# A graph layer on one core: the slot one-hots computed on VectorE instead of ScalarE, and a third batch in the ring of cross one-hots

## The chip, the cores and the metric

The kernel runs on one core of one Trainium2 chip. The metric is the device time of one launch in microseconds (us). The kernel before took 1250.79 us, the median of three runs (1250.07 to 1251.7).

## What is computed

One layer of a graph network with 3125 nodes of 256 features and 53,125 edges (`src`, `dst`, `edge_weight`). In the reference, cut to what matters:

```python
xn = _layernorm(x)
x = x + gnn(xn, src, dst, edge_weight, W, b) + linear_attention_block(xn, ...)
x = x + top2_of_16_experts(_layernorm(x), ...)
# gnn: msgs = edge_weight[:, None] * xn[dst]; agg = segment_sum(msgs, src, 3125); agg @ W.T + b
# attention block: q, k, v; elu + 1; message; norm; 512-wide relu MLP; norm
```

The change lies in the graph part: the sum of the edges' messages over their nodes, and the sorting of edges that comes before it.

## The kernel before, in words

All five engines run their own instruction streams and meet at semaphores. TensorE is called PE, VectorE DVE, ScalarE ACT, GpSimd POOL and SyncE SP in the profile.

There are three stages. In the **first** (to about 118 us), x is normalised, y = xn W is stored to DRAM, and `keys` makes the attention's keys tile by tile: PE multiplies (`project_k`, line 784), ACT makes the exponential in two operations (`exp_keys`, L468 and L470), DVE adds the positive part (L1249) and sums (L1242), PE accumulates (`sum_xk`, L802). There are 25 such tiles. The **middle stage** (about 118 to 785 us) has 13 groups, g = 0 to 12, and each covers 32 edge columns and two tiles of 128 nodes of the dense attention block. The **last stage** is the experts.

A group of the middle stage has 56 steps. In steps 0 to 31 PE multiplies a one-hot matrix (`hot`) by 128 gathered rows of y (L964), and DVE adds the result from PSUM to the node sums in SBUF (`evict_row`, L1319). Steps 32 to 55 are 24 "cross" steps for bins that a tile of edges shares with the next: PE multiplies `cross_hots` by the same rows (L973), and DVE adds two results at a time (`evict_pair`, L1325, at odd steps from 33). DVE makes `hot` eight at a time (L1312), six steps ahead. PE may be four PSUM banks, that is eight row steps, ahead of DVE's evictions. POOL gathers the rows with indirect DMAs (L702), and ACT scales them by the edge weights (`scale_rows`, L530).

Beside these steps each engine has other work, placed at fixed step numbers in a function `beside` of PE and one of DVE, and in a list written out by hand on ACT:

- The dense block of the group: PE's L852 (query), L865 (attend), L876 (turn), L885 (merge), L895 (hidden, at steps 19 to 29) and L904 (`down`, at steps 34 and 35); ACT's `hidden_relu` (L523), of which the second half must be there before PE's step 34; DVE's statistics, centring (L1393) and adding (L1400).
- The sorting of the edges of group g + 2 (`sorts`, so in groups 0 to 10; groups 0 and 1 are sorted in the first stage between the keys). DVE finds each edge's place (L1122 to L1154), splits it into a tile number and a slot number, marks the tile (`mark_tiles`, `in_tile`, L1169, at steps 21, 27, 31, 37) and multiplies the mark by the edge's fields (`make_record`, L1179, at steps 24, 30, 36, 43), eight columns at a time. ACT makes the slot one-hots of the same eight columns (`slot_hot`, L413 and L415): eight operations Abs(iota - slot), one for each column, and one Relu(1 - that). PE multiplies the two (`reorder`, L758, at steps 33, 40, 46, 54). A batch is called k = 0 to 3.
- The cross one-hots (`cross_hot`, L427 and L429) are made by ACT in the same manner, in three batches of eight for each group, into a ring of two batches. So batch 2 of a group can only be written once PE has used batch 0 of the same group (step 39).

On ACT the order in a group, around the change, is: `cross_hot(g, 0)`, scaling, `cross_hot(g, 1)`, `hidden_relu(g, 0)`, scaling twice, `slot_hot(g+2, 0)`, `hidden_relu(g, 1)`, the query's exponential with two table loads, `slot_hot(g+2, 1)`, `slot_hot(g+2, 2)`, `std(1, g)`, `cross_hot(g, 2)`, `slot_hot(g+2, 3)`, scaling three times, `message_turned(g+1)`.

Of the kernel before, what the change touches and what calls it, by code (L numbers as in the profile page):

```python
# [16 lines left out]
P = 128  # L17
# [6 lines left out]
def gps_layer(nc, x, src, dst, edge_weight, gnn_W, gnn_b, Wq, Wk, Wv, Wm, W1, W2, g1, b1, g2, b2,  # L24
# [47 lines left out]
    with ExitStack() as ctx:  # L72
# [3 lines left out]
        def sem(name):  # L76
            return ctx.enter_context(nc.semaphore(name))
# [45 lines left out]

        first_use = sb("first_use", [P, 5 * COLS])
        assert 2 * BATCH * P <= 5 * COLS
# [3 lines left out]
        cross_hots = first_use[:, 0:2 * BATCH * P].rearrange("p (b c) -> p b c", c=P)  # L129
        pieces = sb("pieces", [P, COLS // 2, FIELDS, 2], BF16)  # L130
# [20 lines left out]
        record = [sb(f"record{k}", [P, CH // 2, FIELDS, GT, 2], BF16) for k in range(2)]  # L151
        in_slot = [sb(f"in_slot{k}", [P, CH, P], BF16) for k in range(2)]
        place_b = sb("place_b", [P, GE], BF16)
        place_i = sb("place_i", [P, 3, GE], I32)
        place_f = sb("place_f", [P, GE])
        ends = sb("ends", [BINS, 1])
# [96 lines left out]
        gathered = [[sem(f"gathered{h}_{q}") for q in range(GT // GC)] for h in range(2)]  # L253
        places_ready, slot_hot_ready = sem("places_ready"), sem("slot_hot_ready")
        d_q, d_exp, d_elu, d_att, d_msg = sem("d_q"), sem("d_exp"), sem("d_elu"), sem("d_att"), sem("d_msg")
# [142 lines left out]
        def _(act):  # L398
# [8 lines left out]

            def slot_hot(g, k):
                act.wait_ge(places_ready, g + 1)
                if g * CHUNKS + k >= 2:  # L410
                    act.wait_ge(reordered, g * CHUNKS + k - 1)
                for c in range(CH):
                    act.activation(in_slot[k % 2][:, c, :], iota[:, :], ACT.Abs, bias=place_f[:, k * CH + c:k * CH + c + 1])  # L413
                act.drain()  # L414
                act.activation(in_slot[k % 2][:, :, :], in_slot[k % 2][:, :, :], ACT.Relu, scale=-1.0, bias=1.0).then_inc(slot_hot_ready, 1)  # L415


            def cross_hot(g, b):
                k = g * (CROSS // BATCH) + b
                act.wait_ge(picks_kept, g + 1)  # L420
                if b == 2:
                    act.wait_ge(met, g * STEPS + GT + BATCH)
                elif g >= 1:
                    act.wait_ge(met, (g - 1) * STEPS + GT + (b + 2) * BATCH)
                its = slice(k % 2 * BATCH, (k % 2 + 1) * BATCH)
                for j in range(BATCH):
                    act.activation(cross_hots[:, k % 2 * BATCH + j, :], iota[:, :], ACT.Abs, bias=picked[g % 2][:, b * BATCH + j:b * BATCH + j + 1])  # L427
                act.drain()
                act.activation(cross_hots[:, its, :], cross_hots[:, its, :], ACT.Relu, scale=-1.0, bias=1.0).then_inc(cross_hot_ready, 1)  # L429
# [56 lines left out]
            for t in range(NT):  # L486
                exp_keys(t)
                if t in (1, 3, 5, 7):
# [51 lines left out]
            for g in range(NG):  # L540
                sorts = g + 2 < NG
                more = g + 1 < NG
                if g == 0:
                    scale_rows(0, 2)
                    keep_list(1)
                    scale_rows(0, 3)
                    message_turned(0)
                    scale_rows(0, 4)
                    std(0, 0)
                    first_scaled(0)  # L550
                    scale_rows(0, 5)
                    n1_turned(0)
                    scale_rows(0, 6)
                    scale_rows(0, 7)
                if g >= 1:
                    scale_rows(g, 6)
                    scale_rows(g, 7)
                    std(0, g)
                if g >= 1 and more:
                    keep_list(g + 1)  # L560
                if g >= 1:
                    first_scaled(g)
                    n1_turned(g)
                cross_hot(g, 0)
                if more:
                    scale_rows(g + 1, 0)
                cross_hot(g, 1)
                hidden_relu(g, 0)
                if more:
                    scale_rows(g + 1, 1)  # L570
                    scale_rows(g + 1, 2)
                if sorts:
                    slot_hot(g + 2, 0)
                hidden_relu(g, 1)
                if more:
                    act.preload_act_table(ACT.Exp)
                    query_exp(g + 1)
                    act.preload_act_table(ACT.Sqrt)
                if sorts:
                    slot_hot(g + 2, 1)  # L580
                    slot_hot(g + 2, 2)
                std(1, g)
                cross_hot(g, 2)
                if sorts:
                    slot_hot(g + 2, 3)
                if more:
                    scale_rows(g + 1, 3)
                    scale_rows(g + 1, 4)
                    scale_rows(g + 1, 5)
                    message_turned(g + 1)  # L590
# [48 lines left out]
        def _(pool):  # L639
# [28 lines left out]
            pool.iota(bin_no[:, :, :], [[1, BINS], [0, GE]], base=0, channel_multiplier=0, allow_small_or_imprecise_dtypes=True)  # L668
            pool.iota(tile_of[:, :, :], [[1, GT], [0, 2]], base=0, channel_multiplier=0, allow_small_or_imprecise_dtypes=True)
            pool.iota(tile_start[:, :], [[P, GT]], base=0, channel_multiplier=0, allow_small_or_imprecise_dtypes=True)  # L670
            pool.drain().then_inc(consts_ready, 1)
# [61 lines left out]
        def _(pe):  # L733
# [18 lines left out]
            def reorder(g, k):  # L752
                pe.wait_ge(record_ready, g * CHUNKS + k + 1)
                pe.wait_ge(slot_hot_ready, g * CHUNKS + k + 1)
                if k == 0:
                    pe.matmul(bins_of_tiles, ones[0:BINS, :], meets[:, :], start=True, stop=True)
                for c in range(CH):
                    last = pe.matmul(in_order, in_slot[k % 2][:, c, :], record[k % 2][:, c // 2, :, :, c % 2].rearrange("p f t -> p (f t)"),  # L758
                                     start=(k == 0 and c == 0), stop=(k == CHUNKS - 1 and c == CH - 1))
                last.then_inc(reordered, 1)  # L760
# [189 lines left out]
            def add_up(g):  # L950
# [16 lines left out]
                for b in range(CROSS):  # L967
# [3 lines left out]
                    if b % 2 == 0:  # L971
                        pe.wait_ge(evicted, evictions_before(g, unit))
                    pe.matmul(bank_of(g, unit)[:, (b % 2) * C:(b % 2 + 1) * C], cross_hots[:, (g * CROSS + b) % (2 * BATCH), :],  # L973
                              rows[h][:, bass.ds(row_of[b], 1), :].rearrange("p t c -> p (t c)"),
# [115 lines left out]
        def _(dve):  # L1090
# [57 lines left out]
            def split_places(g):  # L1148
# [15 lines left out]
            def mark_tiles(g, k):  # L1164
                own = slice(k * CH, (k + 1) * CH)
                dve.drain()
                whole = [P, CH // 2, GT, 2]
                two = place_b[:, own].rearrange("p (a b) -> p a b", b=2)
                dve.tensor_tensor(in_tile[:, :, :, :], two.unsqueeze(2).to_broadcast(whole), tile_of[:, :, :].unsqueeze(1).to_broadcast(whole),  # L1169
                                  ALU.is_equal)  # L1170

            def make_record(g, k):
                dve.drain()
                if g * CHUNKS + k >= 2:
# [228 lines left out]
            def beside(g, step):  # L1403
# [327 lines left out]
```

## Time and profile before

| | |
|---|---|
| median of three runs | 1250.79 us (1250.07 to 1251.7) |
| profiled execution, first to last instruction | 1249.4 us |
| PE, DVE, ACT, POOL busy | 1089.0, 800.6, 675.8, 610.4 us |
| mean granted TensorE clock | 0.946 |
| a window of the middle stage, 190 to 707 us: PE, DVE, ACT, POOL busy | 478.71, 441.56, 446.89, 337.56 of 517 us |

For the profiled execution the span is the time on record; no launch time of its own is given with it. It is 1.39 us below the median of the runs. A busy share says how long an engine executed, not whether something else waited for it. An engine can also be unable to go faster with idle time in its row, where its own instructions wait for each other.

### The profile page before, as it was taken

To read this page: it belongs to the slowest core of one execution; us is meant where nothing else is said; L and a number is where in the kernel's file an instruction comes from. 1 tells how busy PE (TensorE), PEld (TensorE's weight loads), DVE (VectorE), ACT (ScalarE), POOL (GpSimd) and SP (SyncE) were. 2 spreads that over 40 slices of the span, in tenths; PEclk is the share of its full clock that TensorE was granted. 3 is DMA by queue.
4 is the path that set the end of the run, shared out by engine and by line. 5 is a ranking of instruction groups with operands and counts; after the bars stand their busy time and mean duration, and the time that the engine had idled before them with its cause. 6 is when DMAs were issued, how large, how long until landed. Compare 5 with 4: busy or idle time off the path is not lost.

```text
span 1249.4 us, 21035 instructions
## 1 busy us (share of the span) xinstructions
PE 1089.0 (87%) x6272; PEld 933.1 (75%) x6272; DVE 800.6 (64%) x1896; ACT 675.8 (54%) x1630; POOL 610.4 (49%) x625
## 2 busy tenths in 40 slices
PE   6797789999999999989999998716999999999990
PEld 5675677777777777767777787306999999999980
DVE  7875678888888888888888877673222222222226
ACT  4568697898978979789797874311011011011000
POOL 5937556575675766757557570002333333333320
PEclk9898899999999999999999999767999999999995
DMA  7214222232222322223223230325999999999958
GB/s 221 87 35 123 68 72 81 72 93 77 85 85 72 93 74 84 89 71 92 76 81 89 75 102 7 103 95 176 335 325 334 331 335 330 330 334 333 335 170 307
DMA packets 113487, 196.08 MB, mean 157 GB/s; under 512 B 13506, under 2 KB 61440, under 8 KB 113408
## 3 DMA queue, kind: packets, MB, share of 16 engines
q1 hardware_dynamic: 84073, 120.62, 28.8%
q0 software_dynamic: 26112, 71.34, 18.2%
q10 hardware_dynamic: 3222, 3.20, 0.7%
q8 instruction: 33, 0.54, 0.2%
q14 instruction: 47, 0.38, 0.1%
HBM read 177.12 MB, written 17.99 MB: 156 GB/s over the span
## 4 chain that ended last, share of the span: by engine, by line
PE 48%; DVE 14%; ACT 14%; issue 6%; DVEq 6%; POOL 6%; DMA 3%; ACTq 3%; SPq 0%; POOLq 0%
PE psum L1058 19%; PE psum L1068 9%; PE psum L964 7%; ACT in_slot L413 6%; POOL arena L702 5%; PE psum L973 3%; DVE agg L1319 2%; ACT first_use L427 2%; PE psum L895 2%; DMA arena<-y_rows,gather_i 2%; DVE agg L1325 2%; PE psum L885 2%; DVE agg L1700 1%; ACTq L414 1%; ACT arena L530 1%
## 5 line engine op out<-in xcount | busy, mean ns | idle before, releaser
L702 POOL DMA_INDIRECT arena<-y_rows,gather_i x416 | 437.5, 1052 | 250.9 <-PE psum L964 78.2
L964 PE MATMUL psum<-arena,hot 128*128 128x256 f32 x832 | 218.3, 393 | 14.9 <-issue 6.5
L635 ACT ACTIVATE arena<-psum 128x512 f32<-128x512 f32 x64 | 38.2, 597 | 327.6 <-PE psum L1058 327.6
L1319 DVE TENSOR_TENSOR agg<-psum,agg 128x256 f32 x416 | 174.6, 420 | 55.1 <-DVE agg L1319 31.0
L964 PEld LDWEIGHTS psum<-arena,hot 128*128 128x128 f32 x832 | 151.3, 192 | 49.7 <-issue 26.8
L1058 PEld LDWEIGHTS psum<-arena 128*128 128x128 f32 x1536 | 181.2, 194 | 4.9 <-issue 2.5
L530 ACT ACTIVATE arena<-arena,listed 128x256 f32<-128x256 f32 x416 | 172.6, 495 | 21.7 <-DMA arena<-y_rows,gather_i 21.7
L1058 PE MATMUL psum<-arena 128*128 128x128 f32 x1536 | 181.7, 277 | 2.0 <-DVE arena L1657 2.0
L973 PE MATMUL psum<-arena,first_use 128*128 x624 | 161.0, 394 | 25.2 <-ACT first_use L429 24.8
L1664 DVE TENSOR_TENSOR arena<-psum,arena 128x512 f32<-128x512 f32 x64 | 44.2, 691 | 204.8 <-PE psum L1058 204.8
L718 POOL DMA_INDIRECT chosen_rows<-arena,back_at x64 | 63.3, 988 | 219.7 <-DVE arena L1671 215.0
L973 PEld LDWEIGHTS psum<-arena,first_use 128*128 128x128 f32 x624 | 115.4, 196 | 48.8 <-issue 35.1
L413 ACT ACTIVATE in_slot<-iota,place_f 128x128 bf16<-128x128 f32 x416 | 126.6, 387 | 4.4 <-DVE place_f L1154 4.2
L713 POOL DMA_INDIRECT xnT<-n_rows,count x64 | 62.1, 970 | 121.8 <-DVEq L1651 101.6
L1325 DVE TENSOR_TENSOR agg<-psum,agg 128x512 f32<-128x512 f32 x156 | 105.8, 678 | 23.4 <-issue 13.4
L427 ACT ACTIVATE first_use<-iota,picked 128x128 f32<-128x128 f32 x312 | 94.9, 389 | 0.0
L1068 PE MATMUL psum<-arena 128*128 128x256 f32 x384 | 90.8, 379 | 0.0
L1068 PEld LDWEIGHTS psum<-arena 128*128 128x128 f32 x384 | 69.2, 190 | 7.4
L1671 DVE COPY arena<-psum 128x256 f32<-128x256 f32 x64 | 27.2, 424 | 60.7 <-PE psum L1068 60.7
L1312 DVE TENSOR_TENSOR hot<-iota,node_in_bin 128x1024 f32<-128x1024 f32 x52 | 63.0, 1212 | 2.5 <-issue 2.5
L1058 PEld LDWEIGHTS psum<-arena,xnT 128*128 128x128 f32 x512 | 59.7, 192 | 0.8
L1179 DVE TENSOR_TENSOR record<-in_tile,pieces 128x1792 bf16<-128x1792 bf16 x52 | 57.3, 1102 | 4.7
(227 smaller groups left out, 1634.7 us busy)
## 6 DMA issues: line engine op xcount, KB each, us to landing
arena<-in_L_ffn_w_dram SPq DMA_DIRECT2D x144, 512.0 KB, 5.8
xnT<-in_L_ffn_w_dram SPq DMA_DIRECT2D x48, 512.0 KB
arena<-y_rows,gather_i POOLq DMA_INDIRECT x416, 2.8
arena<-chosen_rows SPq DMA_DIRECT2D x4, 1280.0 KB, 9.9
y_rows<-w ACTq DMA_DIRECT2D x6, 512.0 KB, 2.9
agg<-in_x_dram SPq DMA_DIRECT2D x4, 640.0 KB, 6.6
n_rows<-arena SPq DMA_DIRECT2D x4, 640.0 KB
out_dram<-agg SPq DMA_DIRECT2D x4, 640.0 KB
```

The source lines that it names most:

```text
L413: act.activation(in_slot[k % 2][:, c, :], iota[:, :], ACT.Abs, bias=place_f[:, k * CH + c:k * CH + c + 1])
L427: act.activation(cross_hots[:, k % 2 * BATCH + j, :], iota[:, :], ACT.Abs, bias=picked[g % 2][:, b * BATCH + j:b * BATCH + j + 1])
L530: last = act.activation(rows[h][:, t, :], rows[h][:, t, :], ACT.Copy, scale=weight[h][:, t:t + 1])
L702: pool.indirect_dma_start(rows[h][:, t, :], None, y_rows, bass.IndirectOffsetOnAxis(ap=gather_i[h][:, t:t + 1], axis=0)).then_inc(gathered ...
L718: pool.indirect_dma_start(chosen_rows, bass.IndirectOffsetOnAxis(ap=back_at[:, n:n + 1], axis=0), e_y[:, n % WS, :], None)\
L964: pe.matmul(bank_of(g, t // 2)[:, (t % 2) * C:(t % 2 + 1) * C], hot[:, (g * GT + t) % HOTS, :], rows[h][:, t, :], start=True, stop=True).t ...
L973: pe.matmul(bank_of(g, unit)[:, (b % 2) * C:(b % 2 + 1) * C], cross_hots[:, (g * CROSS + b) % (2 * BATCH), :], rows[h][:, bass.ds(row_of[b ...
L1058: last = pe.matmul(bank[b][:, m * P:(m + 1) * P], w[s][:, k * EH + m * P:k * EH + (m + 1) * P], e_xT[:, h, k * P:(k + 1) * P], start=(k == ...
L1068: last = pe.matmul(bank[6 + h][:, 0:C], e_hid[:, h, k * P:(k + 1) * P], e_w3[s][:, k * C:(k + 1) * C], start=(k == 0), stop=(k == EHC - 1))
L1312: dve.tensor_tensor(hot[:, first:first + BATCH, :], iota[:, :].unsqueeze(1).to_broadcast([P, BATCH, P]), node_in_bin[g % 2][:, t:t + BATCH ...
L1319: dve.tensor_tensor(own, bank_of(g, t // 2)[:, (t % 2) * C:(t % 2 + 1) * C], own, ALU.add).then_inc(evicted, 1)
L1325: dve.tensor_tensor(own, bank_of(g, GT // 2 + a), own, ALU.add).then_inc(evicted, 1)
```

## The change

1. The slot one-hots move from ACT to DVE. `slot_hot` with its nine ACT operations for eight columns goes. `mark_slots` does the same eight columns in one DVE comparison of 16-bit values, laid out in pairs of columns as `in_tile` already is. Its constant operand `slot_no` is made once by POOL. In groups 0 to 10 it stands at DVE's steps 26, 29, 38 and 44. In the first stage it stands between `mark_tiles` and `make_record` of each batch.
2. The negated float copy of the slot numbers (`place_f`, L1154) goes; `place_b` now holds tile and slot numbers, and one cast writes both.
3. The ring of `cross_hots` holds three batches, so a whole group; a batch waits only for the same batch of the group before. `cross_hot(g, 2)` moves on ACT from behind `std(1, g)` to before `hidden_relu(g, 1)`, into the place of `slot_hot(g+2, 0)`.

```diff
-        first_use = sb("first_use", [P, 5 * COLS])
+        first_use = sb("first_use", [P, CROSS * P])
...
-        in_slot = [sb(f"in_slot{k}", [P, CH, P], BF16) for k in range(2)]
-        place_b = sb("place_b", [P, GE], BF16)
+        in_slot = [sb(f"in_slot{k}", [P, CH // 2, P, 2], BF16) for k in range(2)]
+        slot_no = sb("slot_no", [P, P, 2], BF16)
+        place_b = sb("place_b", [P, 2, GE], BF16)
...
             def cross_hot(g, b):
-                if b == 2:
-                    act.wait_ge(met, g * STEPS + GT + BATCH)
-                elif g >= 1:
-                    act.wait_ge(met, (g - 1) * STEPS + GT + (b + 2) * BATCH)
+                if g >= 1:
+                    act.wait_ge(met, (g - 1) * STEPS + GT + (b + 1) * BATCH)
...
                 if t in (1, 3, 5, 7):
-                    slot_hot(0, t // 2)
...
-                if t in (19, 20, 22, 24):
-                    slot_hot(1, (19, 20, 22, 24).index(t))
...
-                if sorts:
-                    slot_hot(g + 2, 0)
+                cross_hot(g, 2)
                 hidden_relu(g, 1)
...
-                if sorts:
-                    slot_hot(g + 2, 1)
-                    slot_hot(g + 2, 2)
                 std(1, g)
-                cross_hot(g, 2)
-                if sorts:
-                    slot_hot(g + 2, 3)
...
-                dve.tensor_copy(place_b[:, :], place_i[:, 1, :])
-                dve.tensor_scalar(place_f[:, :], place_i[:, 2, :], -1.0, None, ALU.mult).then_inc(places_ready, 1)
+                dve.tensor_copy(place_b[:, :, :], place_i[:, 1:3, :])
...
+            def mark_slots(g, k):
+                if g * CHUNKS + k >= 2:
+                    dve.wait_ge(reordered, g * CHUNKS + k - 1)
+                whole = [P, CH // 2, P, 2]
+                two = place_b[:, 1, k * CH:(k + 1) * CH].rearrange("p (a b) -> p a b", b=2)
+                dve.tensor_tensor(in_slot[k % 2][:, :, :, :], two.unsqueeze(2).to_broadcast(whole), slot_no[:, :, :].unsqueeze(1).to_broadcast(whole),
+                                  ALU.is_equal).then_inc(slot_hot_ready, 1)
...
             def make_records(g, k):
                 mark_tiles(g, k)
+                mark_slots(g, k)
                 make_record(g, k)
...
+                if step == 26 and sorts:
+                    mark_slots(g + 2, 0)
+                if step == 29 and sorts:
+                    mark_slots(g + 2, 1)
+                if step == 38 and sorts:
+                    mark_slots(g + 2, 2)
+                if step == 44 and sorts:
+                    mark_slots(g + 2, 3)
```

## Rows read from the trace of the kernel before

**Rows 1.** The page: each engine's busy time, share and instructions.

```profile
PE 1089.0 (87%) x6272; PEld 933.1 (75%) x6272; DVE 800.6 (64%) x1896; ACT 675.8 (54%) x1630; POOL 610.4 (49%) x625
```

**Rows 2.** Busy by stretch: PE, PEld, DVE, ACT, POOL, clock, DMA share, GB/s.

```profile
190.00:707.00 517.00, 478.71 (x2367) 390.70 (x2366) 441.56 (x1050) 446.89 (x1090) 337.56 (x320) 0.98 0.28 82
346.68:398.30 51.62, 48.45 (x238) 39.80 (x237) 44.13 (x106) 44.77 (x109) 33.40 (x33) 0.97 0.28 82
709.04:750.84 41.80, 40.06 (x189) 33.25 (x188) 30.70 (x71) 29.19 (x69) 31.64 (x32) 1.00 0.34 99
```

**Rows 3.** PE's waits, 190 to 707 us: total, times, longest.

```profile
PE psum L973 <- ACT first_use L429: 21.1, 10, 2.2
PE psum L964 <- issue: 5.8, 10, 0.6
```

**Rows 4.** DVE's waits, 190 to 707 us: total, times, longest.

```profile
DVE agg L1319 <- DVE agg L1319: 22.0, 99, 0.6
DVE agg L1325 <- issue: 13.4, 10, 1.5
DVE agg L1319 <- PE psum L964: 9.7, 39, 0.7
```

**Rows 5.** Timeline of DVE: start, duration, instruction, and idle time before it.

```profile
350.13 0.42 DVE L1319 TENSOR_TENSOR agg<-psum,agg 128x256 f32 x1 [0.21 <-PE psum L964]
350.47 1.22 DVE L1312 TENSOR_TENSOR hot<-iota,node_in_bin 128x1024 f32<-128x1024 f32 x1
351.61 0.42 DVE L1319 TENSOR_TENSOR agg<-psum,agg 128x256 f32 x1
...
369.13 0.42 DVE L1319 TENSOR_TENSOR agg<-psum,agg 128x256 f32 x1 [0.21 <-DVE agg L1319]
369.77 0.42 DVE L1319 TENSOR_TENSOR agg<-psum,agg 128x256 f32 x1 [0.21 <-DVE agg L1319]
...
384.32 0.48 DVE L1393 SCALAR_TENSOR_TENSOR wv<-psum,stat,g2r 128x256 f32<-128x256 f32 x1
384.72 0.68 DVE L1325 TENSOR_TENSOR agg<-psum,agg 128x512 f32<-128x512 f32 x1
```

**Rows 6.** Groups of instructions by shape: busy, mean ns of one, idle before.

```profile
L1312 DVE TENSOR_TENSOR hot<-iota,node_in_bin 128x1024 f32<-128x1024 f32 x52 | 63.0, 1212 | 2.5 <-issue 2.5
L1179 DVE TENSOR_TENSOR record<-in_tile,pieces 128x1792 bf16<-128x1792 bf16 x52 | 57.3, 1102 | 4.7
L1169 DVE TENSOR_TENSOR in_tile<-place_b,tile_of 128x256 bf16<-128x256 bf16 x52 | 16.3, 313 | 4.7
```

**Rows 7.** Timeline of ACT around the second relu.

```profile
366.05 2.43 ACT L413 ACTIVATE in_slot<-iota,place_f 128x128 bf16<-128x128 f32 x8
368.55 1.06 ACT L415 ACTIVATE in_slot<-in_slot 128x1024 bf16<-128x1024 bf16 x1
369.51 0.58 ACT L523 ACTIVATE relu_h<-psum 128x512 f32<-128x512 f32 x1
```

**Rows 8.** Timeline of PE: reorder in a group, and the third cross batch in two groups.

```profile
370.24 0.40 PE L756 MATMUL psum<-meets,ones 25*128 25x32 f32 x2
...
384.84 1.78 PE L973 MATMUL psum<-arena,first_use 128*128 x4 [1.97 <-ACT first_use L429]
...
740.24 1.12 PE L973 MATMUL psum<-arena,first_use 128*128 x4 [0.69 <-ACT first_use L429]
```

**Rows 9.** First stage: timelines of DVE and of PE.

```profile
69.22 0.42 DVE L1249 SCALAR_TENSOR_TENSOR w<-psum,wm 128x256 f32<-128x256 f32 x1 [1.65 <-ACT wm L470]
...
74.20 0.42 DVE L1249 SCALAR_TENSOR_TENSOR w<-psum,wm 128x256 f32<-128x256 f32 x1 [1.64 <-ACT wm L470]
...
83.33 1.13 PE L802 MATMUL psum<-w,arena 128*128 128x256 f32 x4 [0.93 <-DVE w L1249]
...
111.82 1.45 PE L758 MATMUL psum<-record,in_slot 128*128 128x224 bf16 x8 [0.34 <-ACT in_slot L415]
```

**Rows 10.** Timeline of DVE: its wait for ACT in group 0.

```profile
175.18 0.17 DVE L1381 RECIPROCAL stat<-stat 128x2 f32<-128x2 f32 x1 [1.39 <-ACT stat L510]
```

More of the change, by code:

```diff
@@ L122, in gps_layer @@
         relu_h = sb("relu_h", [P, HC, 2 * P])
-        first_use = sb("first_use", [P, 5 * COLS])
-        assert 2 * BATCH * P <= 5 * COLS
+        first_use = sb("first_use", [P, CROSS * P])
+        assert CROSS == 3 * BATCH and 5 * COLS <= CROSS * P
         edge_i = first_use[:, 0:2 * COLS].bitcast(I32).rearrange("p (a c) -> p a c", a=2)
@@ L128, in gps_layer @@
         weight_in = first_use[:, 4 * COLS:5 * COLS]
-        cross_hots = first_use[:, 0:2 * BATCH * P].rearrange("p (b c) -> p b c", c=P)
+        cross_hots = first_use[:, :].rearrange("p (b c) -> p b c", c=P)
         pieces = sb("pieces", [P, COLS // 2, FIELDS, 2], BF16)
@@ L151, in gps_layer @@
         record = [sb(f"record{k}", [P, CH // 2, FIELDS, GT, 2], BF16) for k in range(2)]
-        in_slot = [sb(f"in_slot{k}", [P, CH, P], BF16) for k in range(2)]
-        place_b = sb("place_b", [P, GE], BF16)
+        in_slot = [sb(f"in_slot{k}", [P, CH // 2, P, 2], BF16) for k in range(2)]
+        slot_no = sb("slot_no", [P, P, 2], BF16)
+        place_b = sb("place_b", [P, 2, GE], BF16)
         place_i = sb("place_i", [P, 3, GE], I32)
-        place_f = sb("place_f", [P, GE])
         ends = sb("ends", [BINS, 1])
@@ L253, in gps_layer @@
         gathered = [[sem(f"gathered{h}_{q}") for q in range(GT // GC)] for h in range(2)]
-        places_ready, slot_hot_ready = sem("places_ready"), sem("slot_hot_ready")
+        slot_hot_ready = sem("slot_hot_ready")
         d_q, d_exp, d_elu, d_att, d_msg = sem("d_q"), sem("d_exp"), sem("d_elu"), sem("d_att"), sem("d_msg")
@@ L405, in x_roots @@
                 act.activation(x_root[:, 0, own], x_stat[:, own, 7], ACT.Sqrt, bias=epsc[:, 0:1]).then_inc(std_ready, 1)
[L408 to L415, printed above, removed]
             def cross_hot(g, b):
-                k = g * (CROSS // BATCH) + b
                 act.wait_ge(picks_kept, g + 1)
-                if b == 2:
-                    act.wait_ge(met, g * STEPS + GT + BATCH)
-                elif g >= 1:
-                    act.wait_ge(met, (g - 1) * STEPS + GT + (b + 2) * BATCH)
-                its = slice(k % 2 * BATCH, (k % 2 + 1) * BATCH)
+                if g >= 1:
+                    act.wait_ge(met, (g - 1) * STEPS + GT + (b + 1) * BATCH)
+                its = slice(b * BATCH, (b + 1) * BATCH)
                 for j in range(BATCH):
-                    act.activation(cross_hots[:, k % 2 * BATCH + j, :], iota[:, :], ACT.Abs, bias=picked[g % 2][:, b * BATCH + j:b * BATCH + j + 1])
+                    act.activation(cross_hots[:, b * BATCH + j, :], iota[:, :], ACT.Abs, bias=picked[g % 2][:, b * BATCH + j:b * BATCH + j + 1])
                 act.drain()
@@ L487, in _ @@
                 exp_keys(t)
-                if t in (1, 3, 5, 7):
-                    slot_hot(0, t // 2)
                 if t == 13:
                     keep_list(0)
-                if t in (19, 20, 22, 24):
-                    slot_hot(1, (19, 20, 22, 24).index(t))
             def query_exp(i):
@@ L540, in _ @@
             for g in range(NG):
-                sorts = g + 2 < NG
                 more = g + 1 < NG
@@ L669, in _ @@
             pool.iota(tile_of[:, :, :], [[1, GT], [0, 2]], base=0, channel_multiplier=0, allow_small_or_imprecise_dtypes=True)
+            pool.iota(slot_no[:, :, :], [[1, P], [0, 2]], base=0, channel_multiplier=0, allow_small_or_imprecise_dtypes=True)
             pool.iota(tile_start[:, :], [[P, GT]], base=0, channel_multiplier=0, allow_small_or_imprecise_dtypes=True)
@@ L757, in reorder @@
                 for c in range(CH):
-                    last = pe.matmul(in_order, in_slot[k % 2][:, c, :], record[k % 2][:, c // 2, :, :, c % 2].rearrange("p f t -> p (f t)"),
+                    last = pe.matmul(in_order, in_slot[k % 2][:, c // 2, :, c % 2], record[k % 2][:, c // 2, :, :, c % 2].rearrange("p f t -> p (f t)"),
                                      start=(k == 0 and c == 0), stop=(k == CHUNKS - 1 and c == CH - 1))
@@ L972, in add_up @@
                         pe.wait_ge(evicted, evictions_before(g, unit))
-                    pe.matmul(bank_of(g, unit)[:, (b % 2) * C:(b % 2 + 1) * C], cross_hots[:, (g * CROSS + b) % (2 * BATCH), :],
+                    pe.matmul(bank_of(g, unit)[:, (b % 2) * C:(b % 2 + 1) * C], cross_hots[:, b, :],
                               rows[h][:, bass.ds(row_of[b], 1), :].rearrange("p t c -> p (t c)"),
@@ L1167, in mark_tiles @@
                 whole = [P, CH // 2, GT, 2]
-                two = place_b[:, own].rearrange("p (a b) -> p a b", b=2)
+                two = place_b[:, 0, own].rearrange("p (a b) -> p a b", b=2)
                 dve.tensor_tensor(in_tile[:, :, :, :], two.unsqueeze(2).to_broadcast(whole), tile_of[:, :, :].unsqueeze(1).to_broadcast(whole),
```

## The prediction

> **What bounds the kernel now.** I read the page's busy shares first. PE leads over the span, DVE has only 64% and ACT 54% [rows 1], so at first sight DVE is the natural place for ACT's work. The expert stage, the last third, touches none of the changed lines and weighs on those shares, so I read the middle stage alone. There ACT and DVE are nearly level, 446.89 and 441.56 us busy of 517, and PE has 478.71 [rows 2].
>
> Next the waits. PE's only large one is for ACT's third cross batch: 21.1 us in ten groups, 2.1 us each [rows 3], at 384.84 in the group that I follow [rows 8]. The change goes at exactly this. The question is whether DVE can take what PE is then ready to give. DVE's list of waits answers it. In ten groups it has 22.0 us in 99 waits of an eviction for the eviction before it, and 9.7 us in 39 waits laid to PE, both about 0.22 to 0.25 each; and 1.34 us in each group in front of an L1325, for nothing that the profile shows [rows 4]. The timeline explains the first kind: two evictions in a row start 0.64 us apart, 0.42 of work and 0.21 until the semaphore of the first one counts [rows 5]. The 39 waits are nearly all 0.21 too, the same delay laid to PE: 9.7 - 39 x 0.21 is 1.5 us in ten groups. The 1.34 us stands where DVE loads the next group's 32 bin numbers into registers, its own work.
>
> So in one period, 346.68 to 398.30, DVE is busy 44.13 of 51.62 us [rows 2], and I take the 7.5 us idle as: 13 gaps of 0.21 (2.7), the register load of 1.46, two of 0.29 behind a drain, and 2.7 us of bubbles under 0.1 us. It hardly ever waits for another engine. While PE stood 2 us waiting for ACT, DVE was working off its backlog. PE in turn waits 0.58 us in each group "for issue" [rows 3] at step 16, right behind the end of `hot` (350.47 + 1.22 = 351.69 against 351.79), so for DVE. I conclude that DVE sets the period of groups 1 to 10, at an occupancy of only 85%. A period without sorting, 709.04 to 750.84, has DVE at 30.70 us and falls to 41.80, with PE 96% busy [rows 2]: there PE sets the pace.
>
> **Step 1: the price of one `mark_slots`.** No such operation is in the trace, but `in_tile` is the same comparison with the same pairing, 256 elements in 0.313 us, and `record`, also 16-bit, has 1792 in 1.102 [rows 6]. The slope is 0.789 / 1536 = 0.514 ns an element, so 1024 elements take 0.313 + 768 x 0.000514 = 0.71 us. I take 0.69, since both means hold some slow early ones. Bounds: an operation of 256 elements (0.31) below, and the 32-bit comparison of 1024 elements, `hot`, 1.21 us above [rows 6]; it is nearest to `in_tile` in form.
>
> The Trainium skill bears on this ("VectorE: DVE Perf Modes", The perf-mode tier table): a 16-bit tensor_tensor runs at twice the rate of a 32-bit one and no further. By its 1224 ns for 2048 elements and its fixed 151 cycles at 0.96 GHz an estimate for 1024 is 0.69 us. The trace agrees as far as it goes: `record`, 16-bit, takes 1.10 us for 1792 elements where `hot`, 32-bit, takes 1.21 for 1024 [rows 6].
>
> **Step 2: what it adds to DVE's serial time.** An inserted operation costs less than its length where it fills a semaphore gap. `hot` of 1.22 stands between evictions at 350.13 and 351.61: 1.48 us apart against 0.64 without, so it adds 0.84, which is its length less 0.38 [rows 5]. Steps 26 and 29 are such places (the evictions of 369.13 and 369.77 are those of 26 and 27): 0.69 - 0.38 = 0.31 each. At steps 38 and 44 there is no gap to fill: centring of 0.48 at 384.32, then the pair at 384.72 [rows 5], so only the 0.08 us overlap of neighbours comes off, 0.61 each. Removing `place_f`, whose neighbours start 0.16 apart, and doubling the cast give back some 0.12. Sum per group: 2 x 0.31 + 2 x 0.61 - 0.12 = 1.72 us. Bounds: 0.31 at all four places gives 1.1, full length at all four 2.6.
>
> **Step 3: groups 1 to 10.** 10 x 1.72 = 17.2. DVE's 1.5 us of true waits for PE go, since PE no longer stalls: +15.7 us. PE gets ahead by its 2.1 us, fills its four banks and then waits for evictions. ACT loses 3 x 3.5 us of real work from its critical list.
>
> **Step 4: the moved batch and the new waits.** In front of the second relu on ACT stood `slot_hot(g+2, 0)`, 366.05 to the relu at 369.51 [rows 7]. `cross_hot(g, 2)` has the same nine operations, so the relu, and PE's `down` behind it, come at the same time: nothing. No DMA is issued by what moves; SP's and POOL's queues hold nothing of it. DVE's new wait for `reordered` is for work two batches back, as `record`'s is: nothing. Behind it stand the evictions, so a mistake here would cost at once. On PE, `reorder` now waits for DVE. For k = 0 it starts at 370.24 [rows 8], while the eviction of step 26 ends at 369.55 and `mark_slots` about 0.69 later, 370.2. This is level, with no room. But PE's second `down` ends at 375.7 and DVE's statistics of it start at 377.95, a margin of 2.2 us, so I take nothing.
>
> **Step 5: first stage.** Here ACT does set the pace while slots are made: 4.97 us for two key tiles from 69.22 to 74.20, with DVE waiting 1.65 us for ACT in each [rows 9]. Four operations of `exp_keys` and one `slot_hot` (3.5) are this period. Without it, PE needs 4 x 0.865 + 0.8 = 4.26 us and DVE 4.97 - 1.65 + 0.61 = 3.93. In group 0's sort the list comes some 2.8 us sooner on DVE; PE, next in line, gains 0.7 and the 0.93 us of 83.33 [rows 9], so 1.7. In group 1's sort DVE becomes the bound: from the places (93.8 us) six keys of 0.85, four batches of 1.53 + 0.61 and the last key's sum, about 15.4 us, against 18.0 to the `reorder` at 111.82 [rows 9]: 2.6. Together -4.3 us; bounds -3 and -7, the latter at PE's 4.26 us throughout. All of the middle stage starts from that `reorder`'s list.
>
> **Step 6: ends.** In group 0 DVE does wait, 1.39 us for ACT's square root at 175.18 [rows 10] behind two `slot_hot`; that goes, 1.22 comes at steps 38 and 44, and 0.65 of waiting at 191.63 goes too: -0.8. Groups 11 and 12 sort nothing and lose 0.69 us of PE's stall each, group 11 at 740.24 [rows 8]: -1.3.
>
> **Sum.** 15.7 - 4.3 - 0.8 - 1.3 = +9.3 us. The profiled span goes from 1249.4 to 1258.7; the median, 1.39 above it, to about 1260.
>
> **The rivals.**
> *PE sets the groups, DVE has room (faster).* For it speaks PE's busy share of 93% and the visible stall. The Trainium skill would read it so: "Perfetto Trace Analysis", Identifying the Most-Contended Engine, says that for VectorE and ScalarE occupancy is the measure; this case's rows give ACT slightly more of it than DVE. As a mechanism of this kernel: if the evictions' 0.21 us gaps and bubbles can shrink when PE runs ahead, DVE has up to 7.5 us, and each group falls by the 2.1 us. Then -21 - 2.2 (group 0) - 1.3 - 4.3 = -29, so 1222 us. Against it: 0.21 recurs to the hundredth at every second eviction. It decides if DVE's room is over 1.7 us a group.
> *The two halves cancel (same).* If DVE absorbs about 1.1 us of each 1.72, through the step 16 delay or idle moments that I count as its own, ten groups cost 6 and the ends give 6.4: 1251.
> *The comparison runs at the 32-bit rate (slower still).* Then 1.21 us a piece: 2 x 0.83 + 2 x 1.13 - 0.12 = 3.8 a group, 38 - 1.5 - 6.4 = +30, 1281 us. `in_tile` speaks against it.
> *PE's wait for slots takes over.* If `mark_slots(g+2, 0)` comes over 2.2 us late for `down`, each group grows by the excess; half a us makes it 1265. It is part of my forecast's upper range.
>
> **How the numbers follow.** A difference within 0.2%, 2.5 us, can't be told from none. The forecast with its upper range has a chance of 0.70, PE as the bound 0.15, cancelling 0.11, the 32-bit rate 0.04. The forecast's own range is -6.4 + 9.5 = +3 (1.1 a group) to +19 (2.6 a group, early gain 3), so 1254 to 1270. I reach down to 1247 to take in the cancelling case and cut at 1271; what is left out is most of PE's case and the 32-bit rate. Slower 0.73, same 0.11, faster 0.16.
>
> **What would show it.** Right: `in_slot` on DVE at 0.69 us, L973 no longer waiting for L429, PE waiting for L1319 instead, DVE with no waits but 0.21, and pair statistics of neighbouring groups 53.3 us apart instead of 51.6; group 0 starting 4 us sooner. Wrong: periods of 51.6 or less with DVE busy over 46 us, which means that DVE had room; or long waits of L756 for `in_slot`.

## The result and the profile after

The changed kernel takes 1262.88 us (median of four runs, 1262.56 to 1264.42) against 1250.75 us: a ratio of 1.0101, with a 95% interval of 1.0087 to 1.0116. It is slower by 12.1 us; 9.3 were forecast. The profiled execution spans 1261.2 us (before 1249.4).

The page first, busy time and share of each engine:

```profile
span 1261.2 us, 20504 instructions
PE 1088.5 (86%) x6272; PEld 922.1 (73%) x6272; DVE 829.2 (66%) x1935; ACT 501.1 (40%) x1162; POOL 611.6 (48%) x626
```

ACT lost 175 us of work and DVE gained 28.6 [rows 1]. Counted as work removed this is a large saving, and yet the kernel is slower. Busy time by stretch (PE, PEld, DVE, ACT, POOL, clock, DMA share, GB/s), a window of the groups, one period with sorting, and group 11:

```profile
190.00:707.00 517.00, 467.20 (x2306) 371.42 (x2305) 448.22 (x1034) 306.90 (x719) 330.75 (x314) 1.00 0.27 81
347.11:400.69 53.58, 48.08 (x238) 38.00 (x238) 46.37 (x109) 31.18 (x73) 34.18 (x33) 1.00 0.27 79
721.48:765.90 44.42, 39.84 (x186) 32.66 (x185) 30.73 (x71) 29.67 (x71) 32.29 (x32) 1.00 0.33 96
```

A period has gone from 51.62 to 53.58 us, with DVE 2.24 us busier in it and PE's work the same [rows 2]. PE's granted clock rose from 0.97 to 1.00 in the period and bought nothing. The waits, PE first, then DVE (total, times, longest, 190 to 707 us):

```profile
PE psum L949 <- DVE agg L1309: 16.7, 31, 0.8
PE psum L852 <- DVE wv L1344: 13.1, 9, 1.5
PE psum L940 <- DVE hot L1296: 6.0, 10, 0.9
PE psum L940 <- DVE agg L1303: 5.3, 9, 0.9
PE psum L940 <- issue: 4.9, 9, 0.6
```

```profile
DVE agg L1303 <- DVE agg L1303: 17.3, 82, 0.2
DVE agg L1309 <- PE psum L949: 14.5, 10, 1.5
DVE agg L1303 <- PE psum L940: 8.4, 35, 0.6
```

The 21.1 us that PE waited for ACT's third cross batch [rows 3] are gone. In their place PE waits for DVE: for its evictions (L1309, L1303), for the attention message (L852 behind L1344) and for `hot`. DVE's list has kept its pattern of gaps of 0.21 us [rows 4]. The 14.5 us laid to PE are ten register loads of 1.45; of the same ten, nine were put down to "issue" before: the same stretch under another releaser's name.

The timeline of DVE in one group, the new operations among their neighbours (start, duration, idle before):

```profile
369.57 0.42 DVE L1303 TENSOR_TENSOR agg<-psum,agg 128x256 f32 x1 [0.21 <-DVE agg L1303]
369.92 0.68 DVE L1163 TENSOR_TENSOR in_slot<-place_b,slot_no 128x1024 bf16<-128x1024 bf16 x1
370.51 0.42 DVE L1303 TENSOR_TENSOR agg<-psum,agg 128x256 f32 x1
...
386.11 0.48 DVE L1377 SCALAR_TENSOR_TENSOR wv<-psum,stat,g2r 128x256 f32<-128x256 f32 x1
386.50 0.68 DVE L1163 TENSOR_TENSOR in_slot<-place_b,slot_no 128x1024 bf16<-128x1024 bf16 x1
387.10 0.68 DVE L1309 TENSOR_TENSOR agg<-psum,agg 128x512 f32<-128x512 f32 x1
```

The two evictions of steps 26 and 27 now start 0.94 us apart instead of 0.64 [rows 5]: 0.30 for an operation of 0.68, since it fills the semaphore's gap. At step 44 the pair starts 0.99 us after the centring instead of 0.40: 0.59, and step 38 costs 0.58. The same operation costs twice as much where there is no gap.

The starts of the pair statistics at step 4 (L1354, before L1370) mark the groups. With the start of the last stage's first statistics as the end:

| stretch | before | after | difference |
|---|---|---|---|
| to the pair statistics of group 0 (its step 13) | 136.47 | 131.52 | -4.95 |
| from there to step 4 of group 1 (191.97; 186.77) | 55.50 | 55.25 | -0.25 |
| ten periods to step 4 of group 11 (709.04; 721.48) | 517.07 | 534.71 | +17.64 |
| group 11 (to 750.84; 765.90) | 41.80 | 44.42 | +2.62 |
| group 12 (to 782.97; 796.00) | 32.13 | 30.10 | -2.03 |
| sum | | | +13.03 |

The rest of the span gives 1.2 us back. In the ten periods DVE's busy time rises by 22.1 us (441.91 to 463.98) and its idle time falls by 4.4; that is the 17.6.

### The profile page after: what moved, and what is told of

It reads as the page before. It is cut to its first block, busy times and chain, and to the rows that moved or that the text cites. A ratio compares the mean times of both kernels' runs of the same rounds, so it can differ in the third digit from the quotient of the medians.

```text
span 1261.2 us, 20504 instructions
## 1 busy us (share of the span) xinstructions
PE 1088.5 (86%) x6272; PEld 922.1 (73%) x6272; DVE 829.2 (66%) x1935; ACT 501.1 (40%) x1162; POOL 611.6 (48%) x626
## 3 DMA queue, kind: packets, MB, share of 16 engines
q1 hardware_dynamic: 84073, 120.62, 28.6%
## 4 chain that ended last, share of the span: by engine, by line
PE 55%; DVE 22%; DVEq 13%; issue 6%; ACT 2%; DMA 2%; ACTq 0%; SPq 0%; POOL 0%; POOLq 0%
PE psum L1034 18%; PE psum L940 9%; PE psum L1044 9%; PE psum L871 4%; DVE agg L1303 4%; DVE agg L1309 4%; PE psum L949 3%; DVEq L1141 2%; PE psum L861 2%; DVEq L1148 2%; DVE agg L1692 1%; DVE count L1104 1%; PE psum L734 1%; PE psum L1022 1%; PE psum L828 1%
## 5 line engine op out<-in xcount | busy, mean ns | idle before, releaser
L1303 DVE TENSOR_TENSOR agg<-psum,agg 128x256 f32 x416 | 174.8, 420 | 48.9 <-DVE agg L1303 25.1
L949 PE MATMUL psum<-arena,first_use 128*128 x624 | 161.7, 388 | 17.8 <-DVE agg L1309 17.6
L949 PEld LDWEIGHTS psum<-arena,first_use 128*128 128x128 f32 x624 | 109.7, 190 | 48.1 <-issue 37.6
L1309 DVE TENSOR_TENSOR agg<-psum,agg 128x512 f32<-128x512 f32 x156 | 106.1, 680 | 24.4 <-PE psum L949 19.6
L1296 DVE TENSOR_TENSOR hot<-iota,node_in_bin 128x1024 f32<-128x1024 f32 x52 | 63.1, 1213 | 2.5 <-issue 2.5
L1154 DVE TENSOR_TENSOR record<-in_tile,pieces 128x1792 bf16<-128x1792 bf16 x52 | 57.1, 1099 | 5.1 <-issue 0.4
L1034 PE MATMUL psum<-arena,xnT 128*128 128x128 f32 x512 | 59.7, 275 | 0.0
```

Source lines behind the costliest of these rows:

```text
L1034: last = pe.matmul(bank[b][:, m * P:(m + 1) * P], w[s][:, k * EH + m * P:k * EH + (m + 1) * P], e_xT[:, h, k * P:(k + 1) * P], start=(k == ...
L1296: dve.tensor_tensor(hot[:, first:first + BATCH, :], iota[:, :].unsqueeze(1).to_broadcast([P, BATCH, P]), node_in_bin[g % 2][:, t:t + BATCH ...
L1303: dve.tensor_tensor(own, bank_of(g, t // 2)[:, (t % 2) * C:(t % 2 + 1) * C], own, ALU.add).then_inc(evicted, 1)
L1309: dve.tensor_tensor(own, bank_of(g, GT // 2 + a), own, ALU.add).then_inc(evicted, 1)
```

## The experiments

The theory: in groups 1 to 10 DVE's own chain of instructions, gaps included, sets the period. The main rival: PE sets it through its stall for ACT, and DVE has room for the 1.7 us.

**DVE's price alone.** The kernel before with four comparisons of the new shape, written to a tile that nobody reads; ACT's slot work and PE's stall stay.

```diff
+            def mark_spare(k):
+                whole = [P, CH // 2, P, 2]
+                two = place_b[:, k * CH:(k + 1) * CH].rearrange("p (a b) -> p a b", b=2)
+                dve.tensor_tensor(spare[:, :, :, :], two.unsqueeze(2).to_broadcast(whole), slot_no[:, :, :].unsqueeze(1).to_broadcast(whole),
+                                  ALU.is_equal)
...
+                if step in (26, 29) and sorts:
+                    mark_spare(step // 29)
...
+                if step in (38, 44) and sorts:
+                    mark_spare(2 + step // 44)
```

> The kernel before, whole, with four more VectorE comparisons of the shape of mark_slots in groups 0 to 10, at steps 26, 29, 38 and 44, written to a tile that nobody reads; ScalarE still makes the slot one-hots and TensorE still stalls for the third cross batch. If VectorE's serial work sets the period of the groups, each group grows by 2 x 0.31 + 2 x 0.61 = 1.84 us less 0.15 of waits that go, so +17 to +19 us: about 1268. If TensorE or ScalarE sets it and VectorE has room (the rival), the additions vanish in its idle time and the time stays within 3 us of 1250.8.

Measured: 1267.52 us beside 1251.74, ratio 1.0125 (1.0101 to 1.0148). One period and PE's waits:

```profile
353.06:406.27 53.21, 47.96 (x239) 38.02 (x238) 46.36 (x110) 44.77 (x109) 34.31 (x33) 1.00 0.27 80
```

```profile
PE psum L879 <- DVE wv L1369: 13.1, 9, 1.5
PE psum L976 <- ACT first_use L431: 8.9, 9, 1.5
```

Ten periods take 534.16 us (192.72 to 726.88), 17.1 more than before; 16.9 follow from 1.84 - 0.15 each. This is the experiment that decides. ACT is as loaded as before (44.77 us), its late batch still holds PE up for 1 us a group, down from 2.1, and yet the period is that of the changed kernel, 53.4 against 53.5. So beside these four comparisons the freed ScalarE, the larger ring and the removed stall were worth nothing in the groups, and the rival, whose time was 1222 us, falls. The ring of three batches was in no run by itself.

**The same price twice.** Each `mark_slots` of the groups repeated in the changed kernel.

```diff
+                if g >= 2:
+                    dve.tensor_tensor(in_slot[k % 2][:, :, :, :], two.unsqueeze(2).to_broadcast(whole), slot_no[:, :, :].unsqueeze(1).to_broadcast(whole),
+                                      ALU.is_equal)
+                    dve.drain()
```

> The changed kernel with each mark_slots of groups 0 to 10 done twice, with a drain between. If VectorE sets the period, each repetition costs its full 0.69 us and the drain's bubble, about 0.75, since the gap between evictions is already filled: 4 x 0.75 = 3.0 us a group, 11 groups, +33 us: about 1296. If the changed kernel is held by something else, by a wait of TensorE for the slots for instance, only part of it appears, under 20 us.

Measured: 1297.44 us beside 1251.74, ratio 1.0362 (1.034 to 1.0383). Ten periods take 565.11 us (190.15 to 755.26), 3.04 more each than in the changed kernel. In the trace a repetition starts 0.75 us behind the first:

```profile
383.01 0.68 DVE L1164 TENSOR_TENSOR in_slot<-place_b,slot_no 128x1024 bf16<-128x1024 bf16 x1
383.76 0.69 DVE L1167 TENSOR_TENSOR in_slot<-place_b,slot_no 128x1024 bf16<-128x1024 bf16 x1
```

4 x 0.75 = 3.0: all of what is added appears, the drain included. There is no room left on DVE.

**The gain of the first stage alone.** `mark_slots` for groups 0 and 1 only; from group 2 on, ACT's `slot_hot`, the ring and the order of before.

```diff
-                if t in (1, 3, 5, 7):
-                    slot_hot(0, t // 2)
...
-                if t in (19, 20, 22, 24):
-                    slot_hot(1, (19, 20, 22, 24).index(t))
...
+                if g < 2:
+                    dve.tensor_copy(place_b[:, :, :], place_i[:, 1:3, :])
+                else:
+                    dve.tensor_copy(place_b[:, 0, :], place_i[:, 1, :])
+                    dve.tensor_scalar(place_f[:, :], place_i[:, 2, :], -1.0, None, ALU.mult).then_inc(places_ready, 1)
```

> The slot one-hots are made by VectorE in the first stage only (groups 0 and 1); groups 2 to 12 are sorted with ScalarE's one-hots, with the ring and the order of before. If the first stage gains and the groups lose, this keeps the gain alone: group 0 starts 4.3 to 5 us sooner and all the rest keeps its length, so about 1246 us. If the early gain is given back in group 0 by a transfer or another wait, it stays at 1250.8.

Measured: 1245.16 us beside 1251.74, ratio 0.9951 (0.9934 to 0.9967). The pair statistics of group 0 come at 131.48, 4.99 sooner than before, and ten periods take 517.78 us, 0.7 more than before's. One part of the change is a gain of 5 to 6 us, and it lasts.

**The order of the second relu in groups 11 and 12.** The table shows +2.62 us in group 11, where I had forecast -0.7. The changed kernel's trace there, PE and then DVE:

```profile
744.91 1.99 PE L880 MATMUL psum<-w,relu_h 128*128 128x256 f32 x8 [1.62 <-ACT relu_h L506]
```

```profile
747.37 0.69 DVE L1309 TENSOR_TENSOR agg<-psum,agg 128x512 f32<-128x512 f32 x1 [3.38 <-PE psum L949]
```

```diff
-                cross_hot(g, 2)
+                if sorts:
+                    cross_hot(g, 2)
                 hidden_relu(g, 1)
+                if not sorts:
+                    cross_hot(g, 2)
```

> The changed kernel with one order restored in groups 11 and 12, where nothing is sorted: hidden_relu(g, 1) goes before cross_hot(g, 2) there. I had priced this move at nothing because slot_hot stood in that place before; in these two groups nothing stood there. If that is what the 1.62 us wait of TensorE and the 3.4 us wait of VectorE in group 11 of the changed kernel come from, the time falls by 2.5 to 3 us, to about 1260. If TensorE's own work sets group 11, nothing changes: 1262.9.

Measured: 1263.6 us beside 1251.74, ratio 1.0088 (1.0068 to 1.0108), not told apart from the changed kernel's 1.0101. This trace must be read by stretches: its group 0 comes 2.8 us later than in the changed kernel (134.29 against 131.52), in a part that the edit doesn't touch. PE's wait for the relu is gone, and DVE's falls to this:

```profile
747.85 0.69 DVE L1313 TENSOR_TENSOR agg<-psum,agg 128x512 f32<-128x512 f32 x1 [1.55 <-PE psum L953]
```

Group 11 takes 42.51 us (723.79 to 766.30) instead of 44.42, so 1.9 us come back, and 0.7 over the 41.80 of the kernel before are left, which I haven't traced; but group 12 takes 31.11 (to 797.41) instead of 30.10. The mechanism is as supposed, its worth in the two groups is 0.9 us, and my 2.5 to 3 was too much. In group 12 DVE now waits 0.91 us for a square root of ACT. The changed kernel doesn't wait there, but the kernel before does, and its ACT row says why: the root stands behind a scaling that waits for gathered rows.

```profile
751.99 1.71 ACT L530 ACTIVATE arena<-arena,listed 128x256 f32<-128x256 f32 x4 [3.66 <-DMA arena<-y_rows,gather_i]
```

```profile
753.92 0.16 DVE L1381 RECIPROCAL stat<-stat 128x1 f32<-128x1 f32 x1 [0.98 <-ACT stat L510]
```

In `relu_first` the same scaling waits 3.97 us for the rows, in the changed kernel 2.46. POOL issues the gathers of these groups one behind the other with 0.30 us between them, so a group 11 that ends sooner meets rows that are not there yet. That this is what gives half of the gain back is read from these rows and was not tested.

**The pairing.** The slot one-hots laid out column by column, with the slot number repeated along the innermost axis.

```diff
-                whole = [P, CH // 2, P, 2]
-                two = place_b[:, 1, k * CH:(k + 1) * CH].rearrange("p (a b) -> p a b", b=2)
-                dve.tensor_tensor(in_slot[k % 2][:, :, :, :], two.unsqueeze(2).to_broadcast(whole), slot_no[:, :, :].unsqueeze(1).to_broadcast(whole),
+                whole = [P, CH, P]
+                dve.tensor_tensor(in_slot[k % 2][:, :, :], place_b[:, 1, k * CH:(k + 1) * CH].unsqueeze(2).to_broadcast(whole), slot_row[:, :].unsqueeze(1).to_broadcast(whole),
```

> The changed kernel with the slot one-hots laid out column after column: the slot number is then repeated 128 times along the innermost axis of the comparison instead of standing in pairs. If the pairing is what holds the comparison at 0.69 us, mark_slots takes the time of the 32-bit comparison, about 1.21 us, in_slot's later readers being the same; 44 of them in the groups cost 0.52 us more each, +23 us, and the 8 of the first stage some +2: about 1288. If 16-bit values alone decide, nothing changes: 1262.9.

Measured: 1351.44 us beside 1316.97, ratio 1.0254 (1.0209 to 1.0299). The chip of this comparison and that of the next ones (all but the second run of `mixed_order`) were slower for every kernel, the one before too, by a pause in every group (last section), so I read ratios first. Against the changed kernel's 1.0101 it is 1.5% more, or 19 us of 1251 where 23 to 25 were expected. If the pause costs both kernels the same time, the difference in us is the better measure: 34.5 less 12.1, so 22.4. The groups by shape, `in_slot` here and then in the changed kernel (busy, mean ns):

```profile
L1162 DVE TENSOR_TENSOR in_slot<-place_b,slot_row 128x1024 bf16<-128x1024 bf16 x52 | 63.5, 1221 | 0.0
```

```profile
L1163 DVE TENSOR_TENSOR in_slot<-place_b,slot_no 128x1024 bf16<-128x1024 bf16 x52 | 35.7, 687 | 0.0
```

1221 ns is the duration of the 32-bit `hot` of as many elements (1213). All three operands are 16-bit in both versions; what differs is the innermost step of the slot number, and with it the order of the columns in `in_slot`. PE's multiplications that read it take 263 ns in both. The Trainium skill ("VectorE: DVE Perf Modes", What auto-detection actually checks) asks for 16-bit tensors with a step of one element; the two rows agree with it, 1221 against 687.

**Buying DVE's time back with ACT's.** If DVE is the bound, ACT's freed time should be spent on what costs DVE most. Two of the four `hot` batches of a group go to ACT, made as the cross one-hots are; this version and those that follow also have the order of `relu_first` in groups 11 and 12:

```diff
+            def hot_ahead(g, t):
+                if g >= 1:
+                    act.wait_ge(met, (g - 1) * STEPS + t + 3 * BATCH)
+                act.wait_ge(list_kept, g + 1)
+                for j in range(BATCH):
+                    act.activation(hot[:, t + j, :], iota[:, :], ACT.Abs, scale=-1.0, bias=node_in_bin[g % 2][:, t + j:t + j + 1])
+                act.drain()
+                act.activation(hot[:, t:t + BATCH, :], hot[:, t:t + BATCH, :], ACT.Relu, scale=-1.0, bias=1.0).then_inc(hot_ahead_ready, 1)
...
+                    hot_ahead(g + 1, 0)
                 std(1, g)
+                if more:
+                    hot_ahead(g + 1, BATCH)
```

> The changed kernel, with the first two of the four hot batches of each group made by ScalarE ahead of time (eight Abs and one Relu each), between the query's exponential and the next scaling; and hidden_relu(g, 1) before cross_hot(g, 2) in groups 11 and 12. VectorE loses one hot in the cross steps and one in the row steps, 1.13 + 0.84 = 1.97 us a group. If VectorE sets the period it falls from 53.5 to about 51.5 and the time to 1262.9 - 1 - 11 x 1.97 = about 1240. If TensorE or something else has taken over by then, the period stays above 52.5.

> The same kernel as hot_two, once more, since its first comparison fell on a chip where the kernel before took 1317 us and all engines stood still for some 5 us in every group. On an undisturbed chip: period 51.5 us and about 1240, if VectorE sets the period; above 52.5 and 1252 if not.

Measured: 1310.72 beside 1316.97, ratio 0.9935 (0.9904 to 0.9965), and again 1316.14 beside 1328.39, ratio 0.9913 (0.9881 to 0.9944). Both chips had the pause, so a period of 51.5 was not seen; the ratios answer to some 1241 us of 1250.8 and speak for it. An estimate agrees: its ten periods take 568.8 and 571.3 us in the two traces, and `mixed_order`, further on, takes 5.4 us more a period on a chip with the pause than on one without; less 54 that leaves 51.5 and 51.7 each.

Then the two slot batches that cost DVE 0.6 us each go back to ACT (`mixed`), and the cheap ones stay on DVE:

```diff
+                if sorts:
+                    slot_hot(g + 2, 2)
+                    slot_hot(g + 2, 3)
                 std(1, g)
+                if more:
+                    hot_ahead(g + 1, 0)
+                    hot_ahead(g + 1, BATCH)
...
-                if step == 38 and sorts:
-                    mark_slots(g + 2, 2)
...
-                if step == 44 and sorts:
-                    mark_slots(g + 2, 3)
```

> As hot_two, and the two slot batches that cost VectorE most, k = 2 and 3 at steps 38 and 44, go back to ScalarE, in the place they had before; ScalarE then has as much work in a group as in the kernel before, but other work. VectorE's serial time in a group is before's 51.6 + 0.62 for slots 0 and 1 - 1.97 = 50.3. If it still sets the period, the time is about 1250.8 - 5 (first stage) - 10 x 1.35 - 2 (groups 0 and 11) = about 1230. If ScalarE's order or TensorE's 48 us of work bind first, the period stays near 51.6 and the time near 1243.

Measured: 1307.69 beside 1316.97, ratio 0.9915 (0.9886 to 0.9944), about half of the gain that was expected. ACT's and DVE's waits show a chain that I had made myself:

```profile
ACT in_slot L414 <- PE psum L770: 21.5, 9, 2.8
```

```profile
DVE stat L1403 <- ACT stat L514: 5.5, 8, 2.2
```

`slot_hot` for k = 3 waits for PE's `reorder` of k = 1, and the square root stands behind it. So the order was changed:

```diff
                 if sorts:
                     slot_hot(g + 2, 2)
+                if more:
+                    hot_ahead(g + 1, 0)
+                std(1, g)
+                if sorts:
                     slot_hot(g + 2, 3)
-                std(1, g)
                 if more:
-                    hot_ahead(g + 1, 0)
                     hot_ahead(g + 1, BATCH)
```

> As mixed, with one change of order on ScalarE. In the trace of mixed slot_hot for k = 3 waits up to 2.8 us for TensorE to finish reorder k = 1, and the square root behind it comes 2.2 us late for VectorE. Here one hot batch and the square root go between the two slot batches. If this wait was what kept mixed from its 50.3 us a group, VectorE's wait for the root goes and the period falls to about 50.3 on an undisturbed chip: about 1230 beside a before of 1250.8, a ratio near 0.984. If TensorE binds, the ratio stays at mixed's 0.99.

> The same kernel as mixed_order, once more, to have it beside a kernel before that takes about 1250. On such a chip: periods of 50.3 to 50.6 us and 1225 to 1232 us. If its gain on the other chip came out of the 5 us in every group in which all engines stood still there, it is under 10 us here.

Measured: 1300.78 beside 1328.39, ratio 0.9801 (0.9764 to 0.9839); and on an undisturbed chip 1229.05 us beside 1250.92, ratio 0.9831 (0.9813 to 0.9849). One period of the second run:

```profile
336.77:386.83 50.06, 47.67 (x238) 37.88 (x237) 43.01 (x106) 44.73 (x109) 33.36 (x33) 1.00 0.29 85
```

Ten periods take 503.34 us (185.62 to 688.96), 50.33 each, where DVE's serial sum gave 50.3. This version is 22 us faster than the kernel before and 34 us faster than the change. ACT does as much as before in a period (44.73 against 44.77 us), but makes other one-hots. The ring of three batches is in this version too, and no run separates its share from that of the exchange.

## Why the prediction was right, and where its terms were off

The direction and the mechanism were right. That the total came within 3 us (+12.1 against +9.3) is in part luck: the errors in groups 11 and 12 have opposite signs (+3.3 and -1.3).

- **What bounds.** Right, and shown twice: adding to DVE alone in the kernel before gives the period of the changed kernel, and a second helping costs its full length. A third time from the other side: taking 3.2 us of DVE's serial time out of the changed period (1.97 for two `hot` batches, 1.2 for two slot batches) takes 3.1 us out of it (53.47 to 50.33).
- **Step 1, the duration.** 0.69 us forecast, 0.687 measured.
- **Step 2, the price in the chain.** 0.31 and 0.61 forecast, 0.30 and 0.58 to 0.60 measured. The rebate of 0.12 for `place_f` was too large: from the start of the cast to the eviction behind it 0.25 us went to 0.21, so 0.04. The sum is 1.74 instead of 1.72.
- **Step 3, the groups.** +15.7 forecast, +17.64 measured. The term that failed is the 1.5 us of DVE's true waits for PE that were to go; this rebate did not appear. Most of the 1.5 was nothing that could go in these groups: 0.44 of it is the wait of 0.65 at 191.63, which step 6 counts again for group 0, and 0.64 lies in eight waits of 0.29 in front of the eviction before a group's pair statistics, which the changed kernel has too. The waits of 0.56 us, laid to PE or to the eviction before, did fall from four to one, so by some 1.0 us. Against that, idle moments laid to "issue", register loads aside, rise from four with 1.1 us to six with 2.2, three of them 0.44 to 0.45 long. What these are I haven't tested. The forecast also took 1.34 us for the register load where it summed up the waits; that is a mean of nine loads of 1.46 and one other wait of 0.25, and its own account of the period has the right 1.46.
- **Step 4, the moved batch.** Right for the groups that sort. Wrong for group 11, and it is the clearest error of the prediction: it priced the move by what had stood in that place, `slot_hot`, and in groups 11 and 12 nothing stood there. `relu_first` shows 1.9 us of the 2.6 in group 11, though only 0.9 over groups 11 and 12 together. PE's new wait for the slots never became one: `in_slot` is not in PE's list in the changed kernel, and in `slots_twice` it is, with 0.8 us at most.
- **Step 5, the first stage.** -4.3 forecast, -4.95 measured, -4.99 in `first_dve`. The length of this stage varies between executions: with slots on DVE in it, group 0 comes at 131.48 to 134.29 us in four traces, so the gain is 2 to 5 us by them; the ratio of `first_dve` answers to 6.1 us, with an interval of 4 to 8. The last `reorder` of group 1's sort starts at 106.78 instead of 111.82 [rows 9]; DVE hardly waits for ACT any more, 1.6 us in all.
- **Step 6, the ends.** Group 0: -0.8 forecast, -0.25 measured; the wait of 1.39 us for the root went, but of the 0.65 at its end 0.29 stayed, and an idle moment of 0.45 laid to "issue" is new. Group 12: -0.7 against -2.0; PE's stall of 0.69 went as forecast, and so did DVE's wait of 0.98 for the root, which the forecast hadn't seen. Group 11: -0.7 against +2.6. Together the ends were 2.5 us worse than the sum had them, and the last stage 1.2 us better.
- **The rivals.** PE as the bound: excluded by `before_spare`. Cancelling: there is a gain that works against the loss, but of 5 us against 18. The 32-bit rate: real, where the innermost step isn't one (`unpaired`), and the paired layout avoids it. Occupancy, which the Trainium skill names as the measure for these engines ("Perfetto Trace Analysis", Identifying the Most-Contended Engine), would have put ACT ahead of DVE here, 446.89 us against 441.56 [rows 2]. The measurement says DVE: some 15% of its time are gaps between its own instructions and its register load.

## What to carry to other kernels

An engine whose idle gaps are its own semaphore delays can be full at 85% busy, as DVE was here; before work is moved to it, add that work as a dummy to the kernel as it is and see whether the time moves. A visible stall of another engine is worth little while the engine behind it is only using it to catch up. When an operation moves, price it in each group where the code runs, also where its old neighbour is absent, and where two engines can do the same kinds of work, give the bound one those that fill its gaps.

## What was unexpected

**A slower 16-bit comparison beside GpSimd's additions.** In the first stage of the changed kernel the first three `in_slot` took 0.68, 1.21 and 0.69 us. POOL's and DVE's timelines:

```profile
56.98 5.20 POOL L662 TENSOR_TENSOR agg<-agg,bias_row 128x256 f32<-128x256 f32 x5
```

```profile
56.91 0.68 DVE L1163 TENSOR_TENSOR in_slot<-place_b,slot_no 128x1024 bf16<-128x1024 bf16 x1
57.68 1.44 DVE L1154 TENSOR_TENSOR record<-in_tile,pieces 128x1792 bf16<-128x1792 bf16 x1
...
61.52 1.21 DVE L1163 TENSOR_TENSOR in_slot<-place_b,slot_no 128x1024 bf16<-128x1024 bf16 x1
...
65.90 0.69 DVE L1163 TENSOR_TENSOR in_slot<-place_b,slot_no 128x1024 bf16<-128x1024 bf16 x1
```

The slow one and the slow `record` (1.44 against 1.09 later) start within POOL's 5.2 us of additions, the first `in_slot` 0.07 us before them. The other traces go the same way. In `relu_first`:

```profile
56.89 5.00 POOL L666 TENSOR_TENSOR agg<-agg,bias_row 128x256 f32<-128x256 f32 x5
```

```profile
57.69 1.21 DVE L1167 TENSOR_TENSOR in_slot<-place_b,slot_no 128x1024 bf16<-128x1024 bf16 x1
...
62.45 0.68 DVE L1167 TENSOR_TENSOR in_slot<-place_b,slot_no 128x1024 bf16<-128x1024 bf16 x1
```

That the additions cause it is read from this overlap in time and was not tested.

**A pause in every group on two chips.** Where the kernel before took 1317 and 1328 us, the traces of the other kernels show DVE waiting 3.3 to 6.5 us at the same place in most of groups 1 to 10, here in `mixed`, DVE, PE and POOL:

```profile
441.66 0.99 DVE L1146 SCALAR_TENSOR_TENSOR count<-psum,count 128x800 f32<-128x800 f32 x1 [5.23 <-remote]
```

```profile
438.62 0.38 PE L907 MATMUL psum<-xnT,w 128*128 128x256 f32 x1 [0.49 <-issue]
440.03 0.59 PE L907 MATMUL psum<-xnT,w 128*128 128x256 f32 x2 [1.03 <-issue]
```

```profile
439.02 0.94 POOL L709 DMA_INDIRECT arena<-y_rows,gather_i  x1 [0.30 <-issue]
441.80 0.94 POOL L709 DMA_INDIRECT arena<-y_rows,gather_i  x1 [1.83 <-remote]
```

Two of the expectations above say that all engines stand still for these 5 us; the rows don't bear that out. DVE is idle from 436.4 on, but PE goes from one matrix multiplication to the next with gaps that no semaphore explains, ACT works until 439.59 and then waits 2.20 us, and POOL issues gathers at its usual distance until 439.96. One kernel ran on both kinds of chip: `mixed_order` takes 557.2 us for its ten periods on one of the two, and 503.3 on the undisturbed chip, so 5.4 us more each. Of the 73.6 us between the two spans (1299.1 and 1225.5), 10.4 lie before group 0's pair statistics and 53.9 in the ten periods. What the pause is stays open.
